# Unit-matrix products on TensorE during the waits for the first and last scale of a quantised feed-forward part

## The chip, the cores and the metric

The kernel runs on one core of a Trainium2 chip. The metric is the device time of one execution in microseconds (us); each time shown is the median of several runs. TensorE (PE) multiplies matrices, VectorE (DVE), ScalarE (ACT) and GpSimd (POOL) work on elements, SyncE (SP) issues most DMA transfers. Each engine runs its own program in order, and the programs are tied together by semaphores.

## What is computed

One decoder layer over 32 sequences of 128 rows with 128 features, all in float32: causal self-attention with one head, cross-attention with 16 heads, and a gated feed-forward part whose activations are quantised with scales taken over the whole tensor.

```python
x = x + attn(layernorm(x), W_qkv)
x = x + xattn(layernorm(x), ctx, mask, Wq, ..., bo)
x = x + ffn(layernorm(x), w_gate, w_up, w_down)

def act_qdq(x):                      # one scale for the whole tensor
    qmax = 2.0 ** 15 - 1.0
    scale = jnp.maximum(jnp.max(jnp.abs(x)) / qmax, 1e-12)
    return jnp.clip(jnp.round(x / scale), -qmax - 1.0, qmax) * scale

def ffn(x, w_gate, w_up, w_down):
    x = act_qdq(x)                                       # scale 1
    up = act_qdq(x @ lpbq_dequant(w_up).T)               # scale 3
    gate = act_qdq(x @ lpbq_dequant(w_gate).T)           # scale 2
    sig = fixed_qdq_u16(jax.nn.sigmoid(gate))
    gate = act_qdq(gate * sig)                           # scale 4
    o = act_qdq(gate * up)                               # scale 5
    return o @ lpbq_dequant(w_down).T
```

Each scale is the largest magnitude of a whole tensor, so all of the tensor must be there before the next step can begin.

## The kernel before

The 32 sequences are worked on in NG = 8 groups of GB = 4; a group is 512 columns. Attention ends sequence by sequence near 227 us. The feed-forward part then runs as five stages over the eight groups, one between each pair of scales. FC = 3 is the number of 128-row pieces of the hidden size 384.

**The scales.** DVE takes the largest magnitude per partition (`mx1`), spreads it over 128 columns (`mxw`), PE transposes that (`over_partitions`, its instruction is on line 887), and DVE takes the maximum of the result and makes the scale and the factor `lev`. `over_partitions(n, count, where)` waits for `g_mx` and writes into bank `where`. There are five such calls, numbered by scale.

**PE's order around the first scale.** After the last sequence's projection PE transposes the gate, up and down weights, then waits for `u_xd` and transposes the normalised rows of group 6 into bank 5 (`turn_rows3(5, NG - 2)`, instructions on line 568), waits again and transposes group 7 into bank 0, waits for ScalarE's copies (`u_tca`) and calls `over_partitions(1, 1, 1)`. Meanwhile DVE normalises the last rows (line 1553), takes maxima (1565), makes the scale (1629 to 1644) and rounds the first two groups to levels (1659, 1661, semaphore `a_n3`). The gate products follow, `hidden(g, gateT, (k,))` on line 895: 24 products of 128x128 by 128x512 in fp32, into banks 2 to 7. ScalarE copies each to `G` (line 1173), turns later groups into integers (1165), and DVE takes the maxima (1671).

**The middle.** The up products run twice, once for their maximum and once for their levels (`un`, ScalarE's line 1201), with scales 2, 3 and 4 between. The last of them is the loop that ends with `hidden(7, upT)`.

**PE's order around the last scale.** After `hidden(7, upT)` PE has one thing in its queue, `over_partitions(5, 1, 0)`, and then the down products. In that time ScalarE makes the last levels of the silu (`c_tn`, line 1207) and of up (`c_un`, line 1201); DVE and POOL multiply the two, a part each (DVE's line 1729 counts on `c_od`, POOL's lines 530 and 535 on `c_op`), and DVE takes the maxima (1671). After scale 5 ScalarE turns the products into levels (line 1229 for the four pieces of the first group, 1234 for each later group), DVE casts them to float32 (1767 and 1773, semaphore `d_on`), and PE multiplies: `down` on line 935, 12 products of 128x128 by 128x128 in fp32 for a group, 96 in all. In the trace each fp32 product of this kind has two PE matmul records and each transpose one. DVE adds the result to `X` (line 1777) and SP stores it.

**Semaphores that the change waits for.** `t_xd` counts DVE's last residual additions, `g_lev` the finished scales, `c_tn`, `c_op` and `c_od` are as above. `ident` is the 128x128 unit matrix in float32. Bank 6 is last read, before the feed-forward part, by the residual of sequence 30; bank 1 holds the transposed maxima of scale 4 until `g_lev` is 4.

Of the kernel before, what the change touches and what calls it, by code (L numbers as in the profile page):

```python
# [38 lines left out]
P = 128  # L39
B = 32  # L40
GB = 4
NG = B // GB
# [23 lines left out]
def decoder(nc, x, ctx_in, mask, Wqkv, Wq, bq, Wk, bk, Wv, bv, Wo, bo, w_gate, w_up, w_down, out):  # L66
    with ExitStack() as ctx:
        def sb(name, shape, dt=F32, where=ctx):
            return where.enter_context(nc.sbuf_tensor(name, shape, dt))

        def sem(name):
            return ctx.enter_context(nc.semaphore(name))
# [3 lines left out]
        ident = sb("ident", [P, P])  # L76
# [130 lines left out]
        def bank(n, k=1):  # L207
            return banks[:, n:n + k, :].rearrange("p k t -> p (k t)")
# [16 lines left out]
        S = {n: sem(n) for n in names}  # L225
# [21 lines left out]
        def seq(t, g, b):  # L247
            return t[:, bass.ds(g * GT + b * P, P)]
# [291 lines left out]
        def _(pe):  # L540
# [25 lines left out]
            def transposes(n, src):  # L566
                for b in range(GB):
                    m = pe.transpose(bank(n)[:, b * P:(b + 1) * P], src(b), ident[:, :])  # L568
                return m
# [246 lines left out]
            def turn_rows3(n, g):  # L816
                transposes(n, lambda b: seq(X3, g, b)).then_inc(S["u_t"], 1)
# [58 lines left out]
            turn_weights3(2, 4)  # L876
            pe.wait_ge(S["u_xd"], GB)
            turn_rows3(5, NG - 2)
            pe.wait_ge(S["u_xd"], 2 * GB)
            pe.wait_ge(S["u_tca"], 3)  # L880
            turn_rows3(0, NG - 1)

            def over_partitions(n, count, where):

                pe.wait_ge(S["g_mx"], 2 * n)
                for k in range(count):
                    m = pe.transpose(bank(where)[:, k * P:(k + 1) * P], mxw[:, k, :], ident[:, :])
                m.then_inc(S["g_all"], 1)

            pe.wait_ge(S["u_tca"], 4)  # L890
            over_partitions(1, 1, 1)

            def hidden(g, w, ks=range(FC)):
                for k in ks:
                    m = pe.matmul(bank(2 + FC * (g % 2) + k), w[:, k * P:k * P + P], grp(X3T, g), start=True, stop=True)  # L895
                return m
# [22 lines left out]
            for g in range(NG):  # L919
                if g < 2:  # L920
                    pe.wait_ge(S["b_umx"], NG - 1 + g)
                else:
                    pe.wait_ge(S["c_un"], g - 1)
                hidden(g, upT).then_inc(S["c_u"], 1)
                if g == 0:
                    over_partitions(3, 1, 0)
                if g == 2:
                    over_partitions(4, 1, 1)
            over_partitions(5, 1, 0)


            def down(n, g, b):
# [886 lines left out]
```

## Time and profile before

| | before |
|---|---|
| median of 3 runs | 357.71 us (357.24 to 358.15) |
| the profiled execution | 358.0 us |
| its span, first to last instruction | 356.1 us |
| mean granted TensorE clock in it | 0.957 |
| PE, DVE, ACT, POOL busy, share of span | 84%, 78%, 72%, 50% |
| chain that ended last: PE, DVE, POOL, ACT | 40%, 27%, 12%, 7% |

The times are of single executions; the profile and the trace are of one more. The clock is given as a share of 2.4 GHz. Ends of matmuls are modelled, and pipelined ones overlap, so that a group's busy time can be less than its records' sum. In the lists an instruction stands as its start, its length, its engine and line, what it writes and reads, and in brackets the idle time of its engine just before and what ended that.

### The profile page before, as it was taken

Reading aid. Unit: us, or ns where it says so; the run is one execution under the profiler, and the core shown is the slowest. Engines: PE = TensorE matmul, PEld = TensorE weight load, DVE = VectorE, ACT = ScalarE, POOL = GpSimd, SP = SyncE. Lnnn points to the kernel's source line nnn. Section 1 sums busy time; section 2 is a strip of 40 time slices with the busy share of each in tenths; the row PEclk is TensorE's granted clock in tenths of the full one; section 3 lists DMA queues with packets and bytes.
Section 4 is the critical chain, followed back from the end, with each engine's and each line's share of the span. In section 5 each row is a group of like instructions: output and inputs, shape, how many; then the busy total and the mean of one; then the engine's idle time right before and its main releaser. Section 6 shows DMA issues by size and latency. Waiting matters only on the chain.

```text
span 356.1 us, 9593 instructions
## 1 busy us (share of the span) xinstructions
PE 298.1 (84%) x3621; PEld 197.0 (55%) x3621; DVE 279.1 (78%) x590; ACT 257.2 (72%) x459; POOL 178.8 (50%) x322
## 2 busy tenths in 40 slices
PE   2799999994989999999999999599985668670996
PEld 1477877863646666666666667444432223220996
DVE  6359988874787899898889885747779997898563
ACT  3268888982788888888888888458787756983850
POOL 3568999951225666747657572200047773663000
PEclk9989999997899999999999999969999999896799
DMA  5971257554066610000000000000000000000124
GB/s 144 258 251 32 89 174 215 173 178 123 13 196 193 178 52 2 4 5 5 3 2 4 6 4 2 0 0 0 2 0 0 1 0 0 1 1 0 31 88 120
DMA packets 23752, 22.68 MB, mean 64 GB/s; under 512 B 3545, under 2 KB 21402, under 8 KB 23578
## 3 DMA queue, kind: packets, MB, share of 16 engines
q1 hardware_dynamic: 22170, 21.78, 20.3%
q8 instruction: 29, 0.48, 0.6%
q10 hardware_dynamic: 1536, 0.28, 0.4%
q14 instruction: 17, 0.14, 0.1%
HBM read 15.75 MB, written 6.31 MB: 62 GB/s over the span
## 4 chain that ended last, share of the span: by engine, by line
PE 40%; DVE 27%; POOL 12%; ACT 7%; issue 7%; DMA 4%; SPq 2%; POOLq 0%; DVEq 0%; ACTq 0%
DVE mxs L1671 10%; DVE nm L1446 10%; PE banks L895 7%; PE banks L935 7%; PE banks L645 5%; PE banks L687 5%; PE banks L709 3%; PE banks L575 3%; POOL rstd L366 3%; PE banks L654 3%; PE banks L705 2%; POOL X L399 2%; PE banks L568 2%; DVE G L1729 2%; POOL pickd L385 2%
## 5 line engine op out<-in xcount | busy, mean ns | idle before, releaser
L1446 DVE TENSOR_REDUCE nm<-banks 128x8 f32<-128x1024 f32 x64 | 78.3, 1223 | 11.9 <-PE banks L645 8.3
L1125 ACT ACTIVATE PT<-banks,bmask,vmask 128x1024 f32<-128x1024 f32 x64 | 76.9, 1201 | 1.8
L895 PE MATMUL banks<-X3T,upT 128*128 128x512 f32 x96 | 45.6, 620 | 14.1 <-DVE mxs L1671 9.3
L515 POOL TENSOR_TENSOR G<-ng,sq 128x1536 int32<-128x1536 int32 (+3 forms) x10 | 27.8, 2789 | 41.2 <-DVE sq L1696 41.2
L1671 DVE TENSOR_REDUCE mxs<-G 128x1 f32<-128x1536 int32 (+5 forms) x29 | 41.9, 1467 | 8.1 <-ACT G L1173 8.1
L687 PE MATMUL banks<-PT,VP 128*32 128x128 f32 x1024 | 41.2, 279 | 0.3 <-DVE qlo L1433 0.3
L895 PEld LDWEIGHTS banks<-X3T,upT 128*128 128x128 f32 x96 | 18.0, 197 | 39.8 <-issue 18.1
L645 PE MATMUL banks<-kd,qd 32*128 32x128 f16 x512 | 25.6, 217 | 10.9 <-ACT pT L999 5.2
L969 ACT ACTIVATE h<-X,shift,rstd 128x128 f32<-128x128 f32 x64 | 26.3, 484 | 10.7 <-POOL shift L411 10.7
L453 POOL CAST NM<-nm 128x64 bf16<-128x64 f32 x32 | 7.6, 236 | 46.6 <-DVE nm L1446 46.6
L687 PEld LDWEIGHTS banks<-PT,VP 128*32 128x32 f32 x1024 | 24.1, 109 | 9.0 <-issue 3.6
L645 PEld LDWEIGHTS banks<-kd,qd 32*128 32x128 f16 x512 | 15.3, 93 | 23.4 <-issue 18.0
L649 PE MATMUL banks<-qd,kd 32*128 32x128 f16 x512 | 25.3, 217 | 0.4 <-DVE h L1423 0.4
L895 PE MATMUL banks<-X3T,gateT 128*128 128x512 f32 x48 | 23.8, 660 | 2.0 <-DVE X3T L1661 2.0
L935 PE MATMUL banks<-downT,sig 128*128 128x128 f32 x192 | 23.4, 288 | 2.3 <-DVE sig L1767 2.3
L366 POOL TENSOR_TENSOR rstd<-vare,mhalf 128x4 f32<-128x4 f32 (+2 forms) x25 | 24.8, 994 | 0.7
L654 PE MATMUL banks<-mT,inj 32*128 32x128 bf16 x512 | 24.9, 215 | 0.0
L935 PEld LDWEIGHTS banks<-downT,sig 128*128 128x128 f32 x192 | 23.2, 204 | 2.6 <-DVE sig L1767 2.6
L468 POOL TENSOR_SCALAR X<-X,mvar,rstd 128x128 f32<-128x128 f32 x24 | 19.4, 814 | 0.0
L1173 ACT ACTIVATE G<-banks 128x512 f32<-128x512 f32 x24 | 14.3, 596 | 6.6 <-PE banks L895 6.5
L895 PEld LDWEIGHTS banks<-X3T,gateT 128*128 128x128 f32 x48 | 10.1, 214 | 15.0 <-issue 15.0
L1184 ACT ACTIVATE ng<-G,lev 128x1536 int32<-128x1536 f32 (+2 forms) x9 | 12.9, 1430 | 7.6 <-POOL G L515 5.9
(186 smaller groups left out, 704.2 us busy)
## 6 DMA issues: line engine op xcount, KB each, us to landing
kd<-k_dram SPq DMA_DIRECT2D x32, 128.0 KB, 2.7
qd<-q_dram SPq DMA_DIRECT2D x32, 128.0 KB, 2.7
ctxg<-in_ctx_dram SPq DMA_DIRECT2D x8, 256.0 KB, 3.2
X3T<-m_dram SPq DMA_DIRECT2D x1, 1792.0 KB, 10.5
out_dram<-y SPq DMA_DIRECT2D x7, 256.0 KB, 2.2
X<-in_x_dram SPq DMA_DIRECT2D x3, 512.0 KB, 9.9
k_dram<-khi SPq DMA_DIRECT2D x7, 128.0 KB, 2.0
k_dram<-klo SPq DMA_DIRECT2D x7, 128.0 KB, 2.2
```

What stands on the lines that cost most here:

```text
L366: nc.gpsimd.tensor_tensor(norms[k]["rstd"][:, c], norms[k]["vare"][:, c], mhalf[:, c], ALU.pow).then_inc(S[done], 1)
L515: nc.gpsimd.tensor_tensor(GI[:, c], ng[:, u, part], sq[:, u, part], ALU.mult).then_inc(S["b_t"], 1)
L645: return pe.matmul(bank(j % 2)[:, s * P:(s + 1) * P], qd[rows(j), n // GB, s, n % GB, :], kd[rows(j), n // GB, s, n % GB, :], start=True, ...
L649: pe.matmul(bank(2 + j)[:, s * P:(s + 1) * P], kd[rows(j), n // GB, s, n % GB, :], qd[rows(j), n // GB, s, n % GB, :], start=(s == 0), sto ...
L654: return pe.matmul(bank(2 + j)[:, s * P:(s + 1) * P], inj[rows(j), s, :], mT[rows(j), n % 2, :], start=False, stop=True, skip_group_check= ...
L687: m = pe.matmul(bank(6 + n % 2)[RT * s:RT * s + RT, a * P:(a + 1) * P], VP[:, n % 2, JT * s + 2 * a + k, :], PT[:, a, (NSET * k + s) * P:( ...
L895: m = pe.matmul(bank(2 + FC * (g % 2) + k), w[:, k * P:k * P + P], grp(X3T, g), start=True, stop=True)
L935: m = pe.matmul(bank(n)[:, b * P:(b + 1) * P], on[:, u, c * GT + b * P:c * GT + b * P + P], downT[:, c * P:(c + 1) * P], start=(c == 0), s ...
L969: act.activation(dst[:, b_ * P:(b_ + 1) * P], seq(X, g, b_), ACT.Identity, scale=norms[k]["rstd"][:, b_:b_ + 1], bias=norms[k]["shift"][:, ...
L1125: act.activation(PT[:, a, :], bank(2 + 2 * a, 2), ACT.Exp, bias=bmask[:, n:n + 1], scale=vmask[:, n:n + 1]).then_inc(S["t_exp"], 1)
L1446: V.tensor_reduce(nm[:, n % 2, 2 * NSET * a:2 * NSET * (a + 1)], bank(0, 2).rearrange("p (h m) -> p h m", m=P), AX.X, ALU.max, negate=True ...
L1671: V.tensor_reduce(mxs[:, k, col:col + 1], src, AX.X, ALU.max, apply_absolute_value=True).then_inc(S[done], 1)
```

## The change

A helper `idle_products(n, k)` issues k products of the unit matrix with itself, 128x128 by 128x128 in fp32, into bank n; nobody reads them, and none signals a semaphore. PE calls it nine times, with 46 products in all: 4, 2 and 7 around the first scale into bank 6, and 6, 4, 4, 4, 6 and 9 around the last scale into bank 1. It adds waits on PE: for the second residual (`t_xd`) before the first burst, for `g_lev` 4 before the tail's bursts, and one for each of the first five bursts of the tail. Nothing else is changed.

```diff
             turn_weights3(2, 4)
             pe.wait_ge(S["u_xd"], GB)
             turn_rows3(5, NG - 2)
+
+            def idle_products(n, k):
+
+                for _ in range(k):
+                    pe.matmul(bank(n)[:, 0:P], ident[:, :], ident[:, :], start=True, stop=True)
+
+            pe.wait_ge(S["t_xd"], 2)
+            idle_products(6, 4)
             pe.wait_ge(S["u_xd"], 2 * GB)
             pe.wait_ge(S["u_tca"], 3)
             turn_rows3(0, NG - 1)
+            idle_products(6, 2)
...
             pe.wait_ge(S["u_tca"], 4)
             over_partitions(1, 1, 1)
+            idle_products(6, 7)
...
                 if g == 2:
                     over_partitions(4, 1, 1)
+
+            pe.wait_ge(S["g_lev"], 4)
+            for name, value, k in (("c_tn", NG, 6), ("c_tn", NG + 1, 4), ("c_op", NG - 1, 4), ("c_op", NG, 4), ("c_od", NG, 6)):
+                pe.wait_ge(S[name], value)
+                idle_products(1, k)
             over_partitions(5, 1, 0)
+            idle_products(1, 9)
```

## Rows read from the trace of the kernel before

**Rows 1.** The page's slices, each 8.9 us long: granted TensorE clock in tenths of 2.4 GHz.

```profile
PEclk9989999997899999999999999969999999896799
```

**Rows 2.** Stretches: from:to, length, busy us (instructions) by engine, granted clock, DMA share, GB/s.

```profile
227.00:231.00 4.00, 1.35 (x9) 0.71 (x7) 3.04 (x12) 1.62 (x4) 0.74 (x2) 1.00 0.00 0
231.20:237.90 6.70, 5.82 (x7) 2.52 (x8) 2.52 (x10) 2.97 (x5) 0.00 (x0) 0.50 0.00 0
268.00:272.00 4.00, 1.93 (x6) 0.75 (x5) 4.00 (x4) 2.77 (x2) 3.10 (x2) 1.00 0.00 0
304.00:308.00 4.00, 1.12 (x3) 0.19 (x1) 3.35 (x3) 3.19 (x3) 3.02 (x2) 1.00 0.01 2
318.00:323.00 5.00, 0.11 (x1) 0.00 (x0) 5.00 (x5) 3.83 (x4) 4.01 (x3) 1.00 0.00 2
324.00:333.00 9.00, 3.55 (x15) 3.26 (x16) 6.23 (x14) 4.27 (x6) 0.00 (x0) 0.50 0.01 2
333.00:334.00 1.00, 1.00 (x9) 1.00 (x8) 0.32 (x1) 1.00 (x2) 0.00 (x0) 0.73 0.00 0
```

**Rows 3.** Chain of work that ended last, 231 to 256: start us, us, what.

```profile
232.08 21.20 PE banks L895 x42
...
253.30 0.60 ACT G L1173
```

**Rows 4.** Timeline of PE, 226 to 232: start us, us, instruction, count, [idle before, releaser].

```profile
226.79 0.60 PE L568 MATMUL banks<-ident,X 128*128 128x128 f32 x4
228.52 0.66 PE L568 MATMUL banks<-ident,X 128*128 128x128 f32 x4 [1.13 <-DVE X L1553]
229.80 0.30 PE L887 MATMUL banks<-ident,mxw 128*128 128x128 f32 x1 [0.62 <-DVE mxw L1631]
```

**Rows 5.** Timeline of ScalarE (ACT), 234 to 240.

```profile
234.16 0.60 ACT L1173 ACTIVATE G<-banks 128x512 f32<-128x512 f32 x1 [0.61 <-PE banks L895]
235.87 0.60 ACT L1173 ACTIVATE G<-banks 128x512 f32<-128x512 f32 x1 [1.11 <-PE banks L895]
...
238.07 0.71 ACT L1165 ACTIVATE n3i<-X3T,lev 128x512 int32<-128x512 f32 x1
238.71 0.60 ACT L1173 ACTIVATE G<-banks 128x512 f32<-128x512 f32 x1
239.56 0.60 ACT L1173 ACTIVATE G<-banks 128x512 f32<-128x512 f32 x1 [0.26 <-PE banks L895]
```

**Rows 6.** PE's instructions by line, 223.8 to 230.2: count, busy us, mean ns, idle before.

```profile
L568 PE MATMUL banks<-ident,X 128*128 128x128 f32 x16 | 2.3, 276 | 1.1 <-DVE X L1553 1.1
L835 PE MATMUL banks<-ident,WR 128*128 128x128 f32 x6 | 0.8, 272 | 0.0
```

**Rows 7.** Chain of work that ended last, 324 to 353.

```profile
327.18 0.49 PE banks L887
...
329.93 23.08 PE banks L935 x189
```

**Rows 8.** Timelines of ACT, POOL and DVE, 317 to 338.

```profile
317.10 1.57 ACT L1207 ACTIVATE ng<-G,lev 128x1536 int32<-128x1536 int32 x1
319.64 1.57 ACT L1207 ACTIVATE ng<-G,lev 128x1536 int32<-128x1536 int32 x1 [0.96 <-POOL G L530]
...
320.59 1.80 POOL L530 TENSOR_TENSOR G<-ng,X 128x768 int32<-128x768 int32 x1 [0.98 <-DVE G L1729]
322.36 1.26 POOL L535 TENSOR_TENSOR G<-ng,X 128x512 int32<-128x512 int32 x1
...
323.73 1.21 DVE L1729 TENSOR_TENSOR G<-ng,X 128x1024 int32<-128x1024 int32 x1
...
332.36 0.96 DVE L1773 CAST sig<-ng 128x1536 f32<-128x1536 int32 x1 [1.04 <-ACT ng L1234]
334.68 0.96 DVE L1773 CAST sig<-ng 128x1536 f32<-128x1536 int32 x1 [1.36 <-PE banks L935]
...
337.36 0.96 DVE L1773 CAST sig<-ng 128x1536 f32<-128x1536 int32 x1 [1.06 <-PE banks L935]
```

## The prediction, made before the changed kernel was run

> **What bounds the kernel now.** I read the page's slices first, then the granted clock by stretches, then the chain of work that ended last around the two waits that the change names, and last the single instructions there. The slices show TensorE's clock below full in four places: near 20 us, near 87 us, near 232 us, and twice after 309 us [rows 1]. The change touches the third and the last.
>
> First scale: the clock is 1.00 up to 231 us and 0.50, that is 1.2 of 2.4 GHz, from 231.2 to 237.9 [rows 2]. Ahead of the fall PE had done 1.35 us of work in 4 us [rows 2], in three short bursts [rows 4]. The chain from 232.08 to 253.28 is one piece of PE matmuls, the gate products of L895, and only then ScalarE's last copies and DVE's maxima [rows 3]. So PE's pace sets the end here, and its first 5.8 us run at half speed. ScalarE's copies show this: each follows a pair of matmul records (one fp32 product of 512 columns); the first two start 1.71 us apart, later ones 0.85 us [rows 5].
>
> Last scale: PE is idle from 318.1 until the transpose at 327.18, and its clock is 0.50 from 324 to 333 and only 0.73 on average in the slice from 333 to 334, which puts the rise at 333.5 [rows 2, 7]. The chain until 327 is DVE; from 329.93 it is PE, 189 records of L935 [rows 7]. Here too PE starts cold, for 3.6 us.
>
> The digit of 6 ahead of that, near 310 us, is a stretch in which the chain runs over DVE alone [rows 1]; the change adds nothing there, and I price it at nothing.
>
> **The change, part by part.** It removes and moves nothing. It adds 46 products of the 128x128 unit matrix with itself in fp32, and waits that only pace them. The nearest shape is the 128x128 fp32 product of L935: DVE's casts at 334.68 and 337.36 are each released when PE has finished 12 of them, so one costs 2.68 / 12 = 0.223 us at full clock [rows 8], and, as the copies' spacing doubles when cold, 0.447 us at half clock [rows 5]. The time that the products cost is nothing if each burst ends before the next real instruction can start:
>
> - 4 products behind the transposes of 226.79. Four transposes issue in about 0.5 us (16 of them have 2.3 us of records, which overlap [rows 6]), so the products run from about 227.3 to 228.2; the next transposes start at 228.52, released by DVE [rows 4]. Slack 0.3 us. The wait on the second residual ahead of them is met already: DVE's program has that residual ahead of the rows whose transposes come before the products.
> - 2 products behind those transposes: 229.05 to 229.5, and the transposed maxima can go at 229.80. Slack 0.3 us. These four transposes are not on the chain; the maxima's is.
> - 7 products behind the maxima's transpose: about 229.95 + 1.56 = 231.5 against 232.08. Slack 0.6 us, while DVE makes the scale and rounds the first group.
> - 6, 4, 4, 4 and 6 products, each behind a wait that other engines meet: ScalarE's levels done at 318.7 and 321.2 (its rows start 317.10 and 319.64, 1.57 us each), POOL's products at 322.4 and 323.6, DVE's at 324.9 [rows 8]. They take 1.34, 0.89, 0.89, 0.89 and 1.34 us, so the third and fourth begin and end about when the next is released, and the last ends at 326.3, 0.9 us ahead of the transpose at 327.18. Queued behind these waits are only that transpose and the down products, and neither can go sooner.
> - 9 products behind that transpose: 327.3 + 2.01 = 329.3, against a first down product at 329.93, or 329.75 once the transpose is warm. Slack 0.4 us, the tightest after the first. Without the cover (cold products) it is 4.0 us and 1.6 us late.
>
> Does the clock then hold? No row shows PE on unit products. First scale: PE's work in the 4 us to 231 rises from 1.35 to some 4 - 0.3 - 0.3 = 3.4 us by the list above, and the row from 227 to 231 at 1.35 us was still 1.00 [rows 2]. I take it as held. Last scale: from 318.1 to 327.18 PE gets 24 x 0.223 = 5.4 us of work in 9.1 us. The nearest rows are 268 to 272, with 1.93 of 4 us busy and the clock at 1.00 throughout, and 304 to 308, with 1.12 of 4 us, after which it was 0.50 [rows 2]. The thinnest new stretch, 318.1 to 322.1, has 1.34 + 0.89 = 2.2 of 4 us: on the side of the row that held. I take it as held, with less trust.
>
> A rule speaks against the first part. In the trace PE did mostly transposes from 224 to 230 (16 of rows, 6 of weights) and the granted clock stayed 1.00 up to 231 [rows 2, 6]. The Trainium skill, page "TensorE: Matmul & The Clock Gate", section "Part 4: PE-mode transpose", says that a transpose does not count as PE-busy for the clock. If that held, only the 13 products (2.9 us of work between 227.3 and 232.08) would speak for the clock at the first scale; the forecast sum stays as it is or loses its gate term. The row does not look like the rule, so it gets a small chance (rival C).
>
> What full clock is worth. Gate products: cold from 232.08 to 237.9, so (237.9 - 232.08) / 2 = **2.91 us**. Checked by the copies: the fourth starts at 238.71; warm it would be near 232.08 + 4 x 0.855 + 0.3 = 235.8 [rows 5]. What is late next: per group PE takes 2.57 us, ScalarE three copies and one levels instruction, 3 x 0.60 + 0.71 = 2.5 us, DVE less; the same pace already holds after 238 with PE full, so nothing takes PE's place, and the whole term moves to the end of the gate part, where the chain goes on through DVE's maxima.
>
> Transpose of the last maxima: 0.49 us on the chain at half clock, against 0.30 us for the same one at full clock at 229.80: **0.18 us** [rows 4, 7].
>
> Down products: the first 12 take from 329.93 to 334.68 now. Warm they take 2.68 + 0.1 = 2.8 us, 1.95 us less. But the second group is late next: its cast on DVE runs 332.36 to 333.32, released by ScalarE, not by PE [rows 8]. PE would be through the first group at 332.7 and wait 0.6 us. Group two then ends near 333.36 + 2.68 + 0.1 = 336.15, against 337.36 now: **1.2 us** rather than 1.95. Later groups are paced by PE already (DVE's casts there wait for PE), so 1.2 us reaches the end.
>
> Sum: 2.91 + 0.18 + 1.2 = 4.3 us. The profiled execution took 358.0 us (span 356.1 and 1.9 around it), so it becomes 353.7. It stands 0.3 us above the median of the three runs shown, 357.71, from which the sum gives 353.4. I take **353.5 us**. How long a stretch was cold in the other executions is not shown; the unprofiled runs spread over 0.9 us, which I put on both sides.
>
> **Rivals.**
> B, the last scale's clock falls all the same. For it: the stretch is only 60% filled, and the rows that fell and held are not far apart. Then the gate term alone stays: 357.7 - 2.9 = 354.8. The nine products cost up to 1.6 us there at half clock; against that PE would be at work from 327.2 on, 2.7 us sooner than now, so the rise (3.6 us after the start of work in the trace) would come near 331. From -0.7 to +1.6 us: 354.1 to 356.4, centre 354.8.
> C, the first scale's clock falls (transposes count for nothing). Seven cold products last 3.1 us, from 229.95 to 233.1, and the gate products start 1.0 us late; the tail's 1.4 us stay. 357.7 + 1.0 - 1.4 = 357.3, less up to 1.0 us if the earlier work brings the rise forward: 356.3 to 357.3. Against it: [rows 6].
> D, slower: the unit products stand in PE's queue in front of the real ones, at half clock in both places. It decides when seven cost over 0.6 + 1.56 = 2.1 us and nine over 2.4 us, that is above 0.27 us each; at 0.447 us they push the gate products back by 1.0 and the down products by 1.6 us with no clock gained: 357.7 + 2.6 = 360.3. Against it: PE would be full just ahead of both, which is how the clock came back in every cold stretch of this trace.
> E, the change does what it says but the time is given back: the gate part ends earlier and a later wait on DMA or another engine absorbs it. For the gate term I find none: no transfer is on the chain between 232 and 353. About 357.5.
>
> **How the numbers follow.** A (both held) 0.74, B 0.16, C 0.04, D 0.03, E 0.03. A's own range is 352.5 to 354.4. The range 352.5 to 355.3 holds A and more than half of B. About 0.3% is what a measurement of this kernel can tell from no change, 1.1 us. A and B are faster: 0.90; C and E within: 0.07; D slower: 0.03.
>
> **What would show it.** Right: granted clock 1.00 from 226 to 309 and from 314 to the end; the copies of the gate products 0.855 us apart from the first on; the gate part's last copy 2.9 us nearer to its first product; the maxima's last transpose 0.30 us; the first product of L935 within 0.1 us of DVE's first cast; and a new gap of 0.6 us in PE before the second down group, released by DVE. Wrong: a 0.50 in any slice of those; unit products running into 232.08 or into the down products' start (B, C, D); or a gate part that is shorter while the distance from its end to the end of the kernel grows (E).

## The result

The changed kernel takes 354.72 us (median of 6 runs, 354.09 to 355.35) against 357.25 us for the kernel before in the same session (6 runs): ratio 0.9926, 95% interval 0.9908 to 0.9945, so 2.5 us or 0.7% faster. In a later session it took 355.23 us against 357.96 us, ratio 0.9933 (0.9908 to 0.9959). Forecast were 353.5 us and a gain of 4.2 us. The time lies in the range given, 352.5 to 355.3, but only near its slow end: it is outside the narrower range, 352.5 to 354.4, that was given for the case that the clock holds at both places.

**The clock.** The page of the changed kernel's profiled execution (354.5 us) has two reduced digits side by side around 88 us (one stretch at half clock, cut by the border of two slices) and one near 291 us, and none at the two places that the change touches; compare [rows 1]:

```profile
span 352.6 us, 9778 instructions
...
PEclk9999999998799999999999999999999998999999
```

By stretches (columns as in [rows 2]), before the gate products, at them, before the last transpose, and at the down products:

```profile
226.00:231.00 5.00, 4.58 (x40) 4.21 (x38) 3.94 (x14) 1.96 (x4) 0.74 (x2) 1.00 0.00 0
231.20:237.00 5.80, 5.41 (x13) 2.58 (x14) 4.00 (x11) 4.81 (x8) 0.00 (x0) 1.00 0.00 0
...
314.00:318.00 4.00, 1.70 (x13) 1.54 (x14) 4.00 (x3) 2.86 (x3) 2.62 (x2) 1.00 0.02 6
318.00:323.00 5.00, 4.75 (x36) 4.18 (x36) 5.00 (x6) 1.41 (x2) 2.24 (x2) 1.00 0.00 0
323.80:332.00 8.20, 7.43 (x62) 7.05 (x63) 5.11 (x11) 6.81 (x8) 0.00 (x0) 1.00 0.00 0
```

Where [rows 2] have 0.50, the clock is now 1.00, also ahead of the transpose, in 314 to 318, with 1.70 of 4 us at work.

**The first scale.** Timeline of PE in the changed kernel (answers to [rows 4]; L883 are the unit products, two records each, L896 the maxima's transpose, L905 the gate products):

```profile
226.73 1.06 PE L883 MATMUL banks<-ident 128*128 128x128 f32 x8
228.03 0.66 PE L568 MATMUL banks<-ident,X 128*128 128x128 f32 x4 [0.24 <-DVE X L1569]
228.53 0.61 PE L883 MATMUL banks<-ident 128*128 128x128 f32 x4
229.31 0.30 PE L896 MATMUL banks<-ident,mxw 128*128 128x128 f32 x1 [0.17 <-DVE mxw L1647]
229.44 1.73 PE L883 MATMUL banks<-ident 128*128 128x128 f32 x14
231.59 1.95 PE L905 MATMUL banks<-X3T,gateT 128*128 128x512 f32 x4 [0.41 <-DVE X3T L1677]
```

Each transpose or product of data that PE waits for there is still released by DVE, after a gap of 0.17 to 0.41 us, and the distance from the maxima's transpose to the first gate product is 2.28 us as before. The bursts cost nothing here. The chain's piece on the gate products is shorter; this answers [rows 3]:

```profile
231.59 18.28 PE banks L905 x42
...
249.89 0.61 ACT G L1189
```

18.28 against 21.20 us for the same 42 records: 2.92 us.

**The last scale.** Timeline of PE (L951 are the down products), and of DVE at the second and third down group; they answer [rows 7, 8]:

```profile
315.25 1.58 PE L883 MATMUL banks<-ident 128*128 128x128 f32 x12 [1.61 <-ACT ng L1223]
317.88 5.33 PE L883 MATMUL banks<-ident 128*128 128x128 f32 x36 [1.05 <-ACT ng L1223]
323.79 0.33 PE L896 MATMUL banks<-ident,mxw 128*128 128x128 f32 x1 [0.59 <-DVE mxw L1647]
323.95 2.17 PE L883 MATMUL banks<-ident 128*128 128x128 f32 x18
326.39 2.94 PE L951 MATMUL banks<-downT,sig 128*128 128x128 f32 x24 [0.26 <-DVE sig L1783]
329.84 0.82 PE L951 MATMUL banks<-downT,sig 128*128 128x128 f32 x5 [0.51 <-DVE sig L1789]
...
328.82 0.96 DVE L1789 CAST sig<-ng 128x1536 f32<-128x1536 int32 x1 [1.04 <-ACT ng L1250]
...
332.89 0.96 DVE L1789 CAST sig<-ng 128x1536 f32<-128x1536 int32 x1 [0.98 <-PE banks L951]
```

The transpose is 0.33 us long instead of 0.47, the first down group runs warm, and PE then waits 0.51 us for DVE's cast of the second group, the gap that was forecast.

**What was not forecast** stands at the very end. DVE's last results in the kernel before, and in the changed one:

```profile
351.36 1.23 DVE L1777 SCALAR_TENSOR_TENSOR y<-banks,scale,X 128x512 f32<-128x512 f32 x2 [1.65 <-DMA out_dram<-y]
353.38 0.48 DVE L1777 SCALAR_TENSOR_TENSOR y<-banks,scale,X 128x256 f32<-128x256 f32 x1 [0.79 <-PE banks L935]
```

```profile
346.29 0.75 DVE L1793 SCALAR_TENSOR_TENSOR y<-banks,scale,X 128x512 f32<-128x512 f32 x1 [1.06 <-PE banks L951]
349.32 0.88 DVE L1793 SCALAR_TENSOR_TENSOR y<-banks,scale,X 128x256 f32<-128x256 f32 x2 [2.28 <-DMA out_dram<-y]
```

Before, DVE waited for a store too, but then again for PE, whose last product ended last. Now both halves of the last result are released by a store: `y` has two tiles in turn, and the last group must wait until the store two groups earlier has landed. The chain shows that store as its own piece:

```profile
345.26 4.04 DMA out_dram<-y
```

PE's last down product ends at 348.87 and the span at 352.62, 3.75 us later, against 2.79 us in the kernel before (353.34 to 356.12).

### The profile page after: what moved, and what is told of

It is laid out like the page before. It is cut to its first block, busy times and chain, and to the rows that moved or that the text cites. A ratio compares the mean times of both kernels' runs of the same rounds, so it can differ in the third digit from the quotient of the medians.

```text
span 352.6 us, 9778 instructions
## 1 busy us (share of the span) xinstructions
PE 306.5 (87%) x3713; PEld 205.6 (58%) x3713; DVE 278.6 (79%) x590; ACT 257.2 (73%) x459; POOL 179.3 (51%) x322
## 4 chain that ended last, share of the span: by engine, by line
PE 37%; DVE 28%; POOL 10%; issue 7%; ACT 7%; DMA 6%; SPq 2%; DVEq 0%; POOLq 0%; ACTq 0%
DVE nm L1462 10%; DVE mxs L1687 10%; PE banks L905 7%; PE banks L645 5%; PE banks L687 5%; PE banks L951 4%; PE banks L709 3%; DMA X3T<-m_dram 3%; PE banks L654 3%; PE banks L705 2%; PE banks L575 2%; DVE G L1745 2%; POOL rstd L366 2%; POOL X L399 2%; PE banks L568 2%
## 5 line engine op out<-in xcount | busy, mean ns | idle before, releaser
L905 PE MATMUL banks<-X3T,upT 128*128 128x512 f32 x96 | 45.9, 622 | 12.8 <-DVE mxs L1687 9.3
L905 PEld LDWEIGHTS banks<-X3T,upT 128*128 128x128 f32 x96 | 17.9, 197 | 38.9 <-issue 17.4
L951 PE MATMUL banks<-downT,sig 128*128 128x128 f32 x192 | 22.0, 276 | 0.8 <-DVE sig L1789 0.5
L951 PEld LDWEIGHTS banks<-downT,sig 128*128 128x128 f32 x192 | 21.6, 192 | 1.1 <-DVE sig L1789 0.7
L905 PE MATMUL banks<-X3T,gateT 128*128 128x512 f32 x48 | 20.8, 594 | 0.4 <-DVE X3T L1677 0.4
L654 PEld LDWEIGHTS banks<-mT,inj 32*128 32x128 bf16 x512 | 15.6, 93 | 3.6
L1125 ACT ACTIVATE oT<-banks 128x128 f32<-128x128 f32 x32 | 8.9, 278 | 11.9 <-PE banks L705 11.9
```

Source lines behind the costliest of these rows:

```text
L654: return pe.matmul(bank(2 + j)[:, s * P:(s + 1) * P], inj[rows(j), s, :], mT[rows(j), n % 2, :], start=False, stop=True, skip_group_check= ...
L951: m = pe.matmul(bank(n)[:, b * P:(b + 1) * P], on[:, u, c * GT + b * P:c * GT + b * P + P], downT[:, c * P:(c + 1) * P], start=(c == 0), s ...
```

## The experiments

All of them were timed against the kernel before on their chip. Beside the time I read three distances from each profile: A, from the first gate product to the last maxima's transpose; B, from that transpose to the end of the last down product; C, from there to the end of the span. They are free of what the first 230 us add and differ by from one execution to the next: the first gate product started between 231.1 and 233.4 us in the thirteen profiles, though all but one (the one with products near 80 us) run the same program up to 226 us.

| kernel | A | B | C | ratio to before (95%) |
|---|---|---|---|---|
| before | 95.10 | 26.16 | 2.79 | |
| changed | 92.20 | 25.07 | 3.75 | 0.9926 (0.9908 to 0.9945) |
| changed, second session | 92.22 | 25.07 | 3.58 | 0.9933 (0.9908 to 0.9959) |
| first scale only | 92.18 | 26.57 | 2.79 | 0.9933 (0.9909 to 0.9957) |
| last scale only | 93.79 | 25.07 | 2.79 | 0.9930 (0.9907 to 0.9952) |
| changed, eight y | 92.19 | 25.07 | 2.79 | 0.9881 (0.9859 to 0.9903) |
| changed, eight y, second session | 92.22 | 25.07 | 2.79 | 0.9893 (0.9864 to 0.9922) |
| before, eight y | 93.89 | 27.27 | 2.79 | 0.9991 (0.9971 to 1.0011) |
| eight y and pieces | 92.20 | 25.15 | 2.79 | 0.9890 (0.9865 to 0.9915) |
| the same and 21 products near 80 us | 92.23 | 25.14 | 2.79 | 0.9881 (0.9836 to 0.9926) |
| transposes, first scale only | 92.20 | 26.02 | 2.79 | 0.9935 (0.9914 to 0.9957) |
| last scale only, 18 for 9 | 93.89 | 25.79 | 2.79 | 0.9970 (0.9955 to 0.9985) |
| last scale only, thin bursts | 93.90 | 26.25 | 2.79 | 0.9980 (0.9959 to 1.0002) |

C is the same 2.79 us in eleven of the thirteen profiles; only the two of the changed kernel, with its two output tiles, differ.

**Each part alone.** The calls of the other part are taken out of the changed kernel.

```diff
-            pe.wait_ge(S["g_lev"], 4)
-            for name, value, k in (("c_tn", NG, 6), ("c_tn", NG + 1, 4), ("c_op", NG - 1, 4), ("c_op", NG, 4), ("c_od", NG, 6)):
-                pe.wait_ge(S[name], value)
-                idle_products(1, k)
             over_partitions(5, 1, 0)
-            idle_products(1, 9)
```

That is the edit for the first scale only; the other one takes out the three calls around the first scale and the wait for `t_xd` instead.

> Only the 13 unit products around the first scale; none around the last. Theory 1 (each scale's products buy back the half-clock stretch behind it, and the tail's gain is then partly lost in DVE's wait for an earlier store of y): the gate products run at full clock from their first, 2.9 us shorter than in the profile of before (copies 0.855 us apart throughout), the down products start at half clock as before; 2.2 to 2.9 us faster than before, near 354.7. Theory 2 (the two parts simply add, and the profiled execution of before was cold for longer than the usual one, so that each part is worth less than read): 1.5 to 1.9 us faster.

> Only the 33 unit products around the last scale. Theory 1: clock 1.00 at the down products, last maxima's transpose near 0.3 us, PE done with the down products 1.0 us sooner, but DVE's last results released by the store two groups before and not by PE, so only 0 to 0.6 us of it reach the end: 356.7 to 357.2. Theory 2: the whole 1.0 us reaches the end, 356.2.

Measured: 355.72 us and 355.31 us against 357.88 us, 2.2 and 2.6 us faster. The clock and the distances are as theory 1 has them: each part shortens its own distance. With the first scale's products alone the down products still start cold and take 23.82 us:

```profile
328.00 23.82 PE L946 MATMUL banks<-downT,sig 128*128 128x128 f32 x192 [2.27 <-DVE sig L1778]
```

With the last scale's alone the tail's chain goes over PE to the last result, with no store in it:

```profile
343.97 6.27 PE banks L947 x56
350.23 0.03 issue
350.26 0.48 DVE y L1789
```

Three things differ from theory 1. The gate products were cold for 3.2 us, not 5.8, in the profile of the last-scale kernel (A is 93.79, not 95.10). The last part's gain reached the end in whole: C is 2.79 us. And its measured gain is more than either theory has, and over 1 us more than the 1.1 us that its distance shows (B, from 26.16 to 25.07). The intervals are 0.8 us to each side, so the two times don't tell the parts' sizes apart; the distances do, as far as single profiles go. The two gains add up to 4.7 us, against 2.5 and 2.7 us for both parts together.

**The store of y.** One output tile for each group, and DVE's waits for stores are no longer needed:

```diff
-        y = sb("y", [P, 2, GT], where=late)
+        y = sb("y", [P, NG, GT], where=late)
...
-                if g > 1:
-                    dve.wait_ge(S["d_st%d" % (g % 2)], 16 * (g // 2))
                 result(g, 2 + g % 2, slice(0, GT), g + 1)
-            dve.wait_ge(S["d_st1"], 16 * (NG // 2 - 1))
```

> The changed kernel with one output tile y for each of the eight groups in place of two in turn, so that DVE waits for no store before the last results. Theory 1 (the store's landing, 4.0 us in the changed kernel's profile, holds the last two results back by about 0.85 us): 0.5 to 1.0 us faster than the changed kernel, 353.7 to 354.2, and the first of the last two results starts within 0.1 us of PE's half group. Theory 2 (the store was late in the profiled execution only): no difference from the changed kernel, 354.7.

> The kernel before with eight output tiles y: what that edit is worth without the unit products. In the profile of before DVE waits 1.7 us for a store at 351.4 but then again for PE at 353.4. Theory 1: within 0.3 us of before, since PE still ends last. A gain of 0.5 us or more would say that the store wait was there before the change and is no part of its account.

Measured: 353.73 us, and 357.56 us for the kernel before with the same edit, 0.3 us faster than before with an interval on both sides of none. So no gain of the tiles can be told without the unit products. To compare with the changed kernel in one session, both ran again:

> The changed kernel once more, on the chip and beside the runs of the next ones, to see whether DVE's wait for a store of y is a part of every execution. Theory 1 (it is): PE's last product to the end of the span takes 3.2 us or more, against 2.8 us in the four kernels measured so far, and the kernel is 0.5 to 1.0 us slower than the one with eight output tiles. Theory 2 (it was that one execution's store): 2.8 us, and the same time as with eight tiles within 0.4 us.

> The changed kernel with eight output tiles, beside the changed kernel itself. Theory 1: 0.5 to 1.0 us faster than it. Theory 2: within 0.4 us of it. In both, gate start to down start 94.8 us and the down products 22.5 us in the profile, as in its first run.

Measured: 355.23 and 353.51 us. The last results with eight tiles, each released by PE:

```profile
347.08 0.48 DVE L1793 SCALAR_TENSOR_TENSOR y<-banks,scale,X 128x256 f32<-128x256 f32 x1 [0.59 <-PE banks L951]
348.42 0.48 DVE L1793 SCALAR_TENSOR_TENSOR y<-banks,scale,X 128x256 f32<-128x256 f32 x1 [0.86 <-PE banks L951]
```

and in the changed kernel's second profile:

```profile
350.59 0.88 DVE L1793 SCALAR_TENSOR_TENSOR y<-banks,scale,X 128x256 f32<-128x256 f32 x2 [2.10 <-DMA out_dram<-y]
```

C is 3.58 against 2.79: the wait was there again, 0.8 us of it at the end. A kernel with two tiles need not have it, though. The last-scale kernel has the same tail and no wait. Its stores' landings show why; this is the line on `y`:

```profile
DMA to landing us min/median/max: 1.8/2.2/4.6
```

The median of the nine stores is 2.2 us in twelve of the thirteen profiles (2.4 in the other), the slowest takes 3.5 to 4.7 us, and a slow one costs time only if DVE is about to wait for it. Read store by store, eight profiles have one slow store, somewhere from the first to the fifth: those of before, of before with eight tiles, of the kernels with one part only, and of the one with products near 80 us. The other five, both of the changed kernel, both of the changed kernel with eight tiles and that with the pieces below, have two or three, and one of them is each time the sixth (3.7 to 4.2 us). The last results of a kernel with two tiles wait for just that store. So the wait may well be the rule for the changed kernel and not chance; why the sixth store is slow there, no run shows. The medians differ by 1.0 us (first sessions, each against its own before 1.6 us) and 1.7 us, of which the tail shows 0.8. In the second session's two profiles the first gate product starts at 233.02 us with two tiles and at 231.09 with eight, so 1.9 of the 2.7 us between their spans lie ahead of the first instruction that differs between the two; what makes up the rest of the medians' difference was not placed.

**The second down group's levels.** In the kernel with eight tiles, ScalarE and DVE make group 1's levels in four pieces, as they do group 0's; PE's waits follow.

```diff
+            for b in range(GB):
+                part = slice(b * P, (b + 1) * P)
+                act.activation(oq[:, 1].rearrange("p (c t) -> p c t", c=FC)[:, :, part],
+                               GI[:, FW:2 * FW].rearrange("p (c t) -> p c t", c=FC)[:, :, part], ACT.Copy, scale=lev[:, 4:5]
+                               ).then_inc(S["d_oq"], 1)
```

> As the changed kernel with eight output tiles, and ScalarE and DVE make the second down group's levels in four pieces of 384 columns, as they do the first group's. It tests the step that the second group's levels are late once PE is warm (PE idle 0.5 us, then a fresh start). If so, PE has no gap in front of the second group and the down products take 21.7 to 22.0 us instead of 22.47: 0.5 to 0.7 us faster. If the levels of the third group only become late instead (ScalarE spends 0.5 us more on four pieces), 22.3 to 22.5 us and no gain.

Measured: 353.69 us, and the down products 22.55 us from first to last against 22.47. The gap moved one group on. PE's timeline of that kernel, in a narrow window:

```profile
327.77 3.96 PE L951 MATMUL banks<-downT,sig 128*128 128x128 f32 x34
332.34 0.91 PE L951 MATMUL banks<-downT,sig 128*128 128x128 f32 x6 [0.61 <-DVE y L1800]
```

The chain there goes over ScalarE's pieces from 324.91 to 330.55 and DVE's cast at 330.57. ScalarE's conversions set when the third group may start, and in four pieces the second group's take it 2.03 us where one instruction takes 1.48 us. The second of the two expectations held, with 22.55 us just above its range.

**The same means near 80 us.** In all the other profiles the clock is 0.50 for 6.8 us near 85 us, behind a wait of PE of about 5 us, and in its later part the chain runs over PE. The new products go into the kernel with the pieces.

```diff
             values1(NG - 1)
+            idle_products(0, 21)
             pe.wait_ge(S["t_k0"], 64)
```

> As the kernel with the pieces, and 21 more unit products in PE's wait near 80 us (into bank 0, behind the last values of the self-attention), after which the clock was 0.50 for 3.4 to 7 us in every profile while the chain ran over PE. It asks if the same means works where nobody put it. Theory 1 (the half-clock stretch sets the time there): clock 1.00 near 85 us, the stretch from 85.7 to 91 shortened by 1.0 to 2.6 us, and this reaches the end. Rival: behind it the chain goes over stores, loads and DVE's maxima, and what PE gains there is waited away by 105 us: within 0.4 us of the kernel with pieces.

Measured: 353.58 us, with runs from 351.15 to 356.36, against 353.69. The clock was 1.00 where the others have 0.50; the stretch from 88 to 90 us in this kernel, and from 86 to 88 in the one with eight tiles (second session):

```profile
88.00:90.00 2.00, 2.00 (x19) 2.00 (x20) 1.74 (x3) 1.41 (x4) 0.00 (x0) 1.00 0.00 0
```

```profile
86.00:88.00 2.00, 2.00 (x13) 1.91 (x10) 1.23 (x1) 0.76 (x2) 0.00 (x0) 0.50 0.03 8
```

From the first scores of the cross-attention to the start of its first weighted values, 14.2 us (85.55 to 99.79) became 13.3 us (87.57 to 100.90). PE's own part of it, to the end of its third batch of scores, went from 8.3 to 5.8 us; of these 2.5 us, 0.9 was left. Against the kernel with the pieces, which is the nearer one, it is 7.9 to 5.8 us, and of the 2.1 us 0.5 was left (13.85 to 13.3 us in all). The rest was waited away here:

```profile
94.56 0.75 DVE qlo L1455
95.33 0.32 SPq L294
95.70 3.51 DMA q_dram<-qlo
```

The time does not show the 0.5 to 0.9 us, in runs that spread over 5 us; the rival is nearer, and a gain below 1 us stays open.

**Transposes as filler.** The helper issues transposes of the unit matrix, around the first scale only.

```diff
-                    pe.matmul(bank(n)[:, 0:P], ident[:, :], ident[:, :], start=True, stop=True)
+                    pe.transpose(bank(n)[:, 0:P], ident[:, :], ident[:, :])
...
-            idle_products(6, 7)
+            idle_products(6, 12)
```

> Only around the first scale, and with transposes of the unit matrix in place of the products: 6, 3 and 12 of them (0.13 us each by the trace, so about the same time as 4, 2 and 7 products). Theory T (transposes keep the clock up, as from 224 to 231 in the profile of before): granted clock 1.00 from 226 to 260, gate start to down start near 94.9 us, as with the products alone around the first scale, and its time within 0.5 us. Theory P (transposes count for nothing, which the Trainium skill, page TensorE: Matmul & The Clock Gate, section Part 4: PE-mode transpose, says): the clock falls to 0.50 before or at the gate products as in before, gate start to down start 96.5 to 98 us.

Measured: 355.64 us against 357.78, and A is 92.20. The granted clock before and at the gate products:

```profile
226.00:231.00 5.00, 4.23 (x35) 3.78 (x36) 3.69 (x14) 1.96 (x4) 0.74 (x2) 1.00 0.00 0
231.00:238.00 7.00, 6.33 (x19) 3.01 (x18) 4.90 (x13) 5.19 (x9) 0.00 (x0) 1.00 0.00 0
```

Here all that PE did between 226.3 and 232.2 us was fp32 transposes, and the granted clock stayed 1.00, that is 2.4 GHz. The five profiles with no filler at this place all fell to 0.50 there. Theory T holds, by one profile and by a gain of 2.1 us, the same as with the products alone (2.2 us).

The Trainium skill's statement that transposes don't count as PE-busy in the same way (page "TensorE: Matmul & The Clock Gate", section "Part 4: PE-mode transpose") does not agree with these rows.

**A queue blocked, and bursts too thin.** In the kernel with the last scale's products only, once 18 products in place of the last 9, once 2 products in each of the five bursts before the transpose.

```diff
-            idle_products(1, 9)
+            idle_products(1, 18)
```

```diff
-            for name, value, k in (("c_tn", NG, 6), ("c_tn", NG + 1, 4), ("c_op", NG - 1, 4), ("c_op", NG, 4), ("c_od", NG, 6)):
+            for name, value, k in (("c_tn", NG, 2), ("c_tn", NG + 1, 2), ("c_op", NG - 1, 2), ("c_op", NG, 2), ("c_od", NG, 2)):
```

> Only around the last scale, and with 18 products in place of 9 behind the last maxima's transpose: the price of a blocked queue. 18 x 0.223 = 4.0 us stand against a distance of 2.6 us from that transpose to the first down product. If the queue's order is what costs, the first down product comes 4.1 to 4.2 us after the transpose, 1.5 us late; 0.5 us of it is taken from the gap in front of the second group, so the down stage ends 0.8 to 1.1 us later than with 9, near 356.2. If PE's unused products gave way, nothing would change: 355.3.

> Only around the last scale, with 2 products in each of the first five bursts in place of 6, 4, 4, 4 and 6, and 9 behind the transpose as before: PE works 2.2 us of the 9 us before the transpose. If the long bursts are needed, the clock falls to 0.50 before the transpose as in the kernel before, the transpose takes 0.47 us, the nine products 4 us, and the first down product comes 1.5 us late at either level of the clock: slower than with the full bursts by 0.5 to 2 us. If the nine products alone do it or the thin bursts suffice: clock 1.00 and the same time as with the full bursts, 355.3.

Measured: 356.38 us and 357.29 us, against 355.31 us for the full bursts with 9 (before: 357.78 and 357.88 in the two sessions). The chains, of the first and of the second:

```profile
326.50 0.33 PE banks L893
326.83 4.02 PE banks L883 x36
330.85 21.45 PE banks L947 x192
```

```profile
326.52 0.47 PE banks L893
327.00 3.84 PE banks L883 x18
330.84 21.94 PE banks L947 x192
```

The unit products themselves are on the chain in both, 18 at full clock (36 records) or 9 at half clock (18 records), and push the first down product to 4.2 and 4.1 us after the transpose, from 2.6. With 18, B grows by 0.72 us: 1.6 late, less 0.87 us by which the down products are shorter (21.60 us for 22.47), because the gap of 0.51 us in front of the second group and PE's fresh start behind it are gone. With the thin bursts the clock had fallen ahead of the transpose:

```profile
318.00:321.50 3.50, 1.39 (x8) 1.04 (x8) 3.50 (x4) 2.74 (x4) 2.52 (x2) 1.00 0.01 2
322.00:330.00 8.00, 6.95 (x29) 6.07 (x30) 6.34 (x14) 2.07 (x5) 0.98 (x1) 0.50 0.01 2
```

That is the mechanism of rivals B and D, brought about by the edit: B is 26.25 us, within the 26.02 to 27.27 us of the kernels without products at the last scale.

## Why the prediction was right or wrong

**The mechanism** was right in each step that it named; what it lacked is the store, below. Both stretches run at full clock; the first burst ends ahead of its transposes, the nine ahead of the down products with 0.26 us to spare (forecast 0.4); the cold middle stretch costs nothing: A is 92.2 us in every profile with the first scale held, though the clock fell near 270 and 307 us in some of them and near 291 us in others.

**The gate term** (2.91 us) was exact for the execution that was profiled, 2.92 measured, and by the profiles about 1 us too large for the usual one. In the profile of before the gate products ran cold for 5.8 us; in the four other profiles without products at the first scale it was 3.2 to 3.4 us (A 93.79, 93.89, 93.89, 93.90). These rows of before with eight tiles show it, with the first gate product at 233.40:

```profile
231.30:233.40 2.10, 0.12 (x1) 0.03 (x1) 1.73 (x6) 0.05 (x1) 0.00 (x0) 1.00 0.00 0
233.50:236.90 3.40, 3.40 (x5) 1.34 (x6) 1.58 (x8) 1.89 (x3) 0.00 (x0) 0.51 0.00 0
237.00:243.00 6.00, 6.00 (x15) 2.65 (x15) 3.94 (x4) 5.18 (x9) 0.00 (x0) 1.00 0.00 0
```

Over the five, A is 94.1, and the term 1.9 us. The two kernels with the first part alone gained 2.2 and 2.1 us, which is nearer to 1.9 than to 2.9, though their intervals reach both. I had written that the other executions' cold stretches are not shown, and put 0.9 us of spread around the sum; taking the one that was shown as the middle is the step that failed.

**The tail's terms.** The transpose gave 0.15 us of the forecast 0.18. The down products went from 23.41 to 22.47 us, 0.94 of the forecast 1.2. The cover, the second group's levels on DVE, was read rightly and its gap was 0.51 for 0.6 us; but that group took 3.05 us from start to release (329.84 to 332.89), not 2.78: a start after a wait cost more than the 0.1 us that I gave it (with 18 unit products behind the transpose the gap is gone, and the down products take 0.36 us less than the gap alone explains). Over the four profiles with a cold tail (B 26.16, 27.27, 26.57, 26.02) the mean gain of B is 1.4 us, as forecast for both terms. The profiled execution of before was one of the two milder ones here.

**The missing term** is the store. I looked for a transfer on the chain between 232 and 353 us and found none (E), which was true; the question was which transfer would be next once PE ends sooner, and the row of DVE waiting 1.65 us for a store in the profile of before answered it. It takes 0.96 and 0.79 us in the two profiles of the changed kernel.

**The sum again**: 1.9 + 1.4 - 0.9 = 2.4 us, against 2.5 and 2.7 measured. Without the store, 3.3 us; the kernel with eight tiles is 4.2 and 4.5 us faster than before, so 1 us there is not explained by the three distances. A gate term of 2.9 us would fit those two, but then neither the changed kernel nor the first part alone. So the sizes of the terms stay uncertain by about 1 us.

**Luck.** The gain was forecast at 4.2 us and measured at 2.5. That the time still lies in the range is owed to the part of it from 354.4 to 355.3 us, which was there for rival B, and B did not happen.

**A misreading** without consequence: the digit near 310 us in [rows 1] is an 8, not a 6; what is said of that stretch holds.

**The rivals.** B and D did not come about. The kernel with the thin bursts shows what they look like: with 2.2 us of products ahead of the transpose in place of 5.4 us the clock fell. How many would have been just enough was not measured. C fell with the transposes. E, time given back later, is what happened in part, in its mild form and at the place I had not named.

The fastest kernel of the study is the changed one with eight output tiles: 353.5 to 353.7 us, ratio 0.9881 and 0.9893. The further edits gave nothing that can be told from it.

## What to carry to other kernels

An engine's slow start behind a wait for a whole-tensor scale can be bought back with useless work, if each burst ends before the next real instruction is ready; 1.6 us too many in the queue cost half of what the clock gave at the last scale (0.72 of 1.4 us). Before pricing such a gain, ask of the last stage which wait is the second to end: here an output tile's store, cheap to remove, held a quarter of the gain. And a stretch at half clock that one profile shows can have another length in the next execution: take several before and put their mean in the sum.

## What the runs showed of the hardware

The gate products were cold for 5.8 us in one execution and for 3.2 to 3.4 us in four, with the same program ahead of them. In the one profile with transposes as filler, PE did nothing but fp32 transposes from 226.3 us to the first gate product at 232.2, and the granted clock stayed at 2.4 GHz. Of nine stores of 128 or 256 KB from one queue, the median landed in 2.2 us (2.4 in one profile of thirteen) and the slowest in 3.5 to 4.7 us; which one was slow differed between kernels, but it was the sixth, among others, in all five profiles of the kernels with both parts and none near 80 us.
